# Macaron block on one core: the two leading bf16 parts of the near position bias, stacked in the array's rows and added with a doubled identity

## The chip, the core and the metric

The kernel runs on one core of one Trainium2 chip. The metric is device time in microseconds (us) of one execution, lower being better. The five engines are TensorE (PE, with its weight loads shown as PEld), VectorE (DVE), ScalarE (ACT), GpSimd (POOL) and SyncE (SP), which here issues nearly all DMAs.

## What is computed

Three stages run one after the other over 4 batches of 1024 tokens with 128 channels: half a feed-forward block, an attention with a relative position bias, half a feed-forward block again. Each feed-forward block holds an attention of its own without bias and a mixture of 8 experts, so all three stages have a 16-head attention over 1024 tokens; only the middle one has the bias.

```python
x = x + 0.5 * _L0_ffn_ref(_layernorm(x), ...)
x = x + _L0_attn_ref(_layernorm(x), ...)      # the middle stage
x = x + 0.5 * _L0_ffn_ref(_layernorm(x), ...)

# in _L0_attn_ref
scores = jnp.einsum('bhqd,bhkd->bhqk', q, k) * scale
scores = scores + compute_bias(N, N, rel_bias_table)   # depends on key - query alone
attn = jax.nn.softmax(scores, axis=-1)
```

The bias of a head depends on key minus query, and is constant beyond a distance of 128.

## The kernel before

**Units and steps.** The attention of one batch and four heads (a quad) is a unit: 16 units a stage, 48 in all, numbered u. A unit has 16 steps t, one for each half of the queries (512 columns) and key tile of 128 keys; a step has two half steps, each with two heads. The global step is 16 u + t. All engines run the same loop over the steps; their waits on semaphores bind them together.

**A half step on PE** (`pe_step`). First two products for the row maximum of work that lies 13 steps ahead (`pe_max`, L1024: 48 rows of the array, 128 columns of weights, 512 columns streamed), into one of two double-bank slots that DVE empties (`dve_max`, by a plain maximum, L1379, or by adding a strip of bias and taking the maximum, L1384). Then two products for the transposed scores of two heads (`pe_score`, L1051), one in rows 0 to 63 of the array and one in rows 64 to 127, each into one of three banks that ACT empties with the exponential (L1273). In the middle stage, where the key tile lies near the queries, the near bias follows (`pe_near`, L1072). Then the products of the weights with the values (`pe_pv`, L1089: 128 rows, 9 columns, four heads in four column strips of the array, 8 fp32 passes in all). The negated row maxima come through `carry_max` on SP, which waits for POOL's `pool_parts` (L806 and after) and carries them over DRAM into the rows of the queries.

**The near bias** (`pe_near`, L1072). The bias of a key tile and the queries up to 96 columns to either side is kept as three bf16 parts (`near`, with axes v, s, j, c: two patterns, three parts, four heads, 320 columns). Each part of each key half (64 keys) is added to the scores by a 64 by 64 product with an identity. The four quarters of the array are used by two heads and two key halves: head s, key half `keys` stands in rows `keys ^ s`, so that the four products of one part lie in four quarters. That makes 12 products for a pair of heads:

```python
for part_ in range(3):
    for s in range(2):
        for keys in range(2):
            rows_ = slice((keys ^ s) * P // 2, (keys ^ s) * P // 2 + P // 2)
            mm_ = pe.matmul(bank[keys half], ident_b[rows_, rows_], near[...][rows_, kt % 2, part_, ...])
```

Steps 0 to 4 and 11 to 15 of a unit have the near bias, ten of sixteen.

**Where the parts come from.** During the first stage the table is built once. For each quad, `cut_near` (SP, eight DMAs) loads a cut, `pool_near` (POOL, L795 to L798) reorders it into `near_all[1]`, and `keep_near` (SP, L618, eight DMAs of one step each) stores it to DRAM in the layout that the quarters need. `NEAR_STEPS` sets the steps at which POOL does this: 61, 85, 109, 125 for the four quads. A quad's cuts are issued in the 8 steps that end two before its step, its keeps in the 8 steps from 7 after it. `pool_near` of a quad waits until all keeps of the quad before have landed. In the middle stage `load_near` reads one quad a unit ahead, in eight DMAs. SP, POOL and PE go through their instructions in order, so `pool_near` stands in POOL's way of what comes next there: `pool_heads` (L822, which PE's output projection L1157 waits for) and `pool_parts` (L806).

Of the kernel before, what the change touches and what calls it, by code (L numbers as in the profile page):

```python
# [18 lines left out]
QUADS = H // 4  # L19
KT = N // P  # L20
HALF = 512
# [17 lines left out]
MARGIN = 96  # L39
NEAR = MARGIN + P + MARGIN  # L40
# [115 lines left out]
STRIP_CUTS = 4  # L156

NEAR_STEPS = [8 * w + 5 for w in (WINDOWS - 1, WINDOWS + 2, WINDOWS + 5, WINDOWS + 7)]
CUT_LOADS = 8


UNIT_LOADS, NEAR_LOADS, STRIP_LOADS = (6, 7, 8, 9, 10, 14), (0, 1, 2, 3, 6, 7, 8, 9), (10, 11, 14, 15)
# [120 lines left out]
def stages(nc, k, x, out):  # L283
    c, w = k.consts, k.w
# [2 lines left out]
    near_in = [k.sem(f"a_near_in{p}") for p in range(2)]  # L287
    near_cut, near_set, near_kept = k.sem("near_cut"), k.sem("near_set"), k.sem("near_kept")
    sheared = [k.sem(f"sheared{quad}") for quad in range(QUADS)]
    strips_cut, ident_ready = k.sem("strips_cut"), k.sem("ident_ready")  # L290
    filled, drained, far_added, row_maxed = k.sem("filled"), k.sem("drained"), k.sem("far_added"), k.sem("row_maxed")
    max_turned = k.sem("max_turned")
    max_parts, max_out, max_rows = k.sem("max_parts"), k.sem("max_out"), k.sem("max_rows")
    max_chain, scored, taken, pv = k.sem("max_chain"), k.sem("scored"), k.sem("taken"), k.sem("pv")
# [29 lines left out]
    turned, max_rest = k.sb("max_turned", [P, 32]), k.sb("max_rest", [P, 32])  # L324
    row_parts = k.sb("max_parts", [P, 3, 32], BF16)
    ident_b = k.sb("ident_b", [P, P], BF16)
    strips = [k.sb(f"strips{p}", [P, 4, STRIP], BF16) for p in range(2)]
    near_all = [k.sb(f"near{p}", [P, NEAR_SET * NEAR], BF16) for p in range(2)]
    near = [t[:, :].rearrange("p (v s j c) -> p v s j c", v=2, s=3, j=4) for t in near_all]
# [61 lines left out]
    taken_bank, heads_bank = k.psum[4:7], k.psum[7]  # L391
# [218 lines left out]
    def keep_near(sp, quad, piece):  # L610


        sp.wait_ge(near_set, quad + 1)
        by_head = lambda tile: tile.rearrange("p (o j s c) -> p s (o j) c", s=2, j=2, c=NEAR)
        src, dst = by_head(near_all[1][:, :]), by_head(k.nears[quad])
        s, p = piece % 2, piece // 2 * 32
        at = (p + s * P // 2) % P
        sp.dma_start(dst[at:at + 32, s], src[p:p + 32, s]).then_inc(near_kept, 16)  # L618

    def store_parts(sp, n, b, h):  # L620

# [98 lines left out]
    def sp_between(sp, step):  # L720
# [11 lines left out]
        for quad in range(QUADS):  # L732
            since = step - NEAR_STEPS[quad]
            if -1 - CUT_LOADS <= since < -1:
                cut_near(sp, quad, since + 1 + CUT_LOADS)
            if 7 <= since < 15:
                keep_near(sp, quad, since - 7)
        if step % KT == 2 and KT < step <= STEPS + 2:
            store_heads(sp, step // KT - 1)
# [46 lines left out]
    def pool_near(pool, quad):  # L786

        pool.wait_ge(near_cut, (quad + 1) * CUT_LOADS * 16)  # L790
        if quad:
            pool.wait_ge(near_kept, quad * 8 * 16)
        strip = lambda v, c0, c1: near_one[:, v, :, :, c0:c1].rearrange("p s j c -> p (s j) c")
        from_cut = lambda v, c0, c1: cut[:, c0:c1, v * 12:(v + 1) * 12].rearrange("p c e -> p e c")
        pool.tensor_copy(strip(0, 0, MARGIN), from_cut(1, 0, MARGIN))  # L795
        pool.tensor_copy(strip(0, MARGIN, NEAR), from_cut(0, MARGIN, NEAR))
        pool.tensor_copy(strip(1, 0, MARGIN + P), from_cut(1, 0, MARGIN + P))
        pool.tensor_copy(strip(1, MARGIN + P, NEAR), from_cut(0, MARGIN + P, NEAR)).then_inc(near_set, 1)  # L798
# [257 lines left out]
    def pe_near(pe, u, e):  # L1056

        half, kt = divmod(e // 4, KT)  # L1060
        if e == 0:
            pe.wait_ge(near_in[u % 2], ((u - B * QUADS) // 2 + 1) * len(NEAR_LOADS) * 16)
            pe.wait_ge(ident_ready, 1)
        for part_ in range(3):
            for s in range(2):
                bank = taken_bank[seat["exp", u, e + s] % 3]
                for keys in range(2):
                    rows_ = slice((keys ^ s) * P // 2, (keys ^ s) * P // 2 + P // 2)
                    at = kt * P + keys * P // 2 - MARGIN
                    lo, hi = max(at, half * HALF), min(at + P // 2 + 2 * MARGIN, (half + 1) * HALF)  # L1070
                    c0 = lo - (kt * P - MARGIN)
                    mm_ = pe.matmul(bank[keys * P // 2:(keys + 1) * P // 2, lo - half * HALF:hi - half * HALF],  # L1072
                                    ident_b[rows_, rows_], near[u % 2][rows_, kt % 2, part_, (e + s) % 4, c0:c0 + hi - lo],
                                    start=False, stop=part_ == 2)
                if part_ == 2:
                    mm_.then_inc(scored, 1)

    def pe_pv(pe, step, part_):

# [591 lines left out]
    with nc.Block() as block:  # L1671
        @block.sync
        def _(sp):
# [12 lines left out]
            for step in range(LAST_STEP):  # L1686
                u, t = divmod(step, UNIT_STEPS)
                if u < UNITS:
# [3 lines left out]
                    if t == LAG + 1:  # L1692
                        carry_max(sp, u, 1)
                        if u + 2 < UNITS and is_mid(u + 2) and not is_mid(u):
                            sp.wait_ge(strips_cut, QUADS * STRIP_CUTS * 16)
                            sp.wait_ge(near_kept, QUADS * 8 * 16)
                    if t == LAG + KT + 1 and u + 1 < UNITS:
                        carry_max(sp, u + 1, 0)
                    pace(sp, step)
# [36 lines left out]
        def _(act):  # L1736
# [9 lines left out]
                act.activation(bias[:, n * 512:(n + 1) * 512], k.psum[n][0:H, :], ACT.Copy).then_inc(bias_sb, 1)  # L1746
            act.wait_ge(weights_in, 12 * 16)
            act.activation(tri_b[:, :], tri[:, :], ACT.Copy).then_inc(ident_ready, 1)
            for step in range(LAST_STEP):
                u, t = divmod(step, UNIT_STEPS)  # L1750
                for i in range(2):
# [118 lines left out]
```

## Time and profile before

| | |
|---|---|
| median of 3 runs | 2491.53 us (2486.31 to 2499.0) |
| the profiled execution | 2491.56 us |
| its span in the profile | 2489.8 us |
| PE busy | 2260.1 us, 91% of the span |
| PEld busy | 844.6 us, 34% |
| DVE busy | 1940.7 us, 78% |
| ACT busy | 1947.4 us, 78% |
| POOL busy | 809.2 us, 33% |

Busy time is the union of an engine's instructions. Those of PE are pipelined: two that follow one another overlap, so the duration of one product says less than the distance between the starts of two groups. A shape such as "64*64 64x256" on a product means rows by columns of the array, then rows by streamed columns; x12 is the number of instructions merged in the row.

### The profile page before, as it was taken

To read this page: it belongs to the slowest core of one execution; us is meant where nothing else is said; L and a number is where in the kernel's file an instruction comes from. 1 tells how busy PE (TensorE), PEld (TensorE's weight loads), DVE (VectorE), ACT (ScalarE), POOL (GpSimd) and SP (SyncE) were. 2 spreads that over 40 slices of the span, in tenths; PEclk is the share of its full clock that TensorE was granted. 3 is DMA by queue.
4 is the path that set the end of the run, shared out by engine and by line. 5 is a ranking of instruction groups with operands and counts; after the bars stand their busy time and mean duration, and the time that the engine had idled before them with its cause. 6 is when DMAs were issued, how large, how long until landed. Compare 5 with 4: busy or idle time off the path is not lost. (4 is left out here: it accounts for less than half of the span.)

```text
span 2489.8 us, 62168 instructions
## 1 busy us (share of the span) xinstructions
PE 2260.1 (91%) x24154; PEld 844.6 (34%) x24154; DVE 1940.7 (78%) x3200; ACT 1947.4 (78%) x3559; POOL 809.2 (33%) x1083
## 2 busy tenths in 40 slices
PE   4899898999998999999899999999999999989935
PEld 1232222235421334543233333332222223542425
DVE  7888898985788887578887988998989998569210
ACT  1698798899887778887677877888979989878822
POOL 1363634320634612032353023023062222062153
PEclk7899999999999999999999999999999999999967
DMA  5346443236215445743544444311212113722525
GB/s 151 108 151 195 144 95 96 68 107 171 73 36 139 120 130 151 217 122 104 140 110 144 120 114 114 76 38 57 54 30 79 45 27 107 199 51 67 138 78 144
DMA packets 293533, 268.11 MB, mean 108 GB/s; under 512 B 62220, under 2 KB 238924, under 8 KB 293208
## 3 DMA queue, kind: packets, MB, share of 16 engines
q1 hardware_dynamic: 281976, 255.76, 37.5%
q0 software_dynamic: 11264, 8.40, 1.9%
q8 instruction: 190, 3.11, 0.5%
q14 instruction: 103, 0.84, 0.1%
HBM read 192.30 MB, written 84.02 MB: 111 GB/s over the span
## 5 line engine op out<-in xcount | busy, mean ns | idle before, releaser
L1273 ACT ACTIVATE probs<-psum 128x512 f32<-128x512 f32 x3072 | 1657.7, 599 | 314.2 <-PE psum L1051 169.9
L1379 DVE TENSOR_REDUCE maxes<-psum 128x2 f32<-128x1024 f32 x1216 | 1424.1, 1216 | 266.2 <-PE psum L1024 263.7
L1089 PE MATMUL psum<-probs,v_ones 128*9 128x256 f32 (+1 forms) x11520 | 945.0, 400 | 0.0
L1024 PE MATMUL psum<-k_staged,q_staged 48*128 48x512 bf16 x3072 | 613.2, 395 | 95.6 <-DVE maxes L1379 57.6
L1051 PE MATMUL psum<-q_staged,k_staged 51*128 51x512 bf16 (+1 forms) x3072 | 632.2, 384 | 35.0 <-DMA q_staged<-neg_max 18.7
L1384 DVE CUSTOM_DVE_ANT_0 biased<-psum,strips 128x512 bf16<-128x512 f32 x640 | 411.7, 686 | 110.9 <-PE psum L1024 89.3
L1024 PEld LDWEIGHTS psum<-k_staged,q_staged 48*128 48x128 bf16 x3072 | 147.9, 93 | 776.2 <-DVE maxes L1379 404.7
L806 POOL CAST max_parts<-max_turned 128x32 bf16<-128x32 f32 x96 | 21.4, 223 | 973.1 <-DVE max_turned L1422 973.1
L1051 PEld LDWEIGHTS psum<-q_staged,k_staged 51*128 51x128 bf16 (+1 forms) x3072 | 259.4, 95 | 193.6 <-ACT probs L1273 62.7
L1089 PEld LDWEIGHTS psum<-probs,v_ones 128*9 128x9 f32 x11520 | 171.1, 88 | 384.6 <-issue 301.7
L1072 PE MATMUL psum<-near,ident_b 64*64 64x256 bf16 (+4 forms) x3840 | 149.3, 252 | 0.0
L950 POOL DMA_INDIRECT x_tokens<-expert_out,rows x64 | 100.3, 1567 | 59.3 <-DMA expert_out<-m_out 41.5
L822 POOL TENSOR_TENSOR o_heads_t<-values,weight_recips 128x512 f32<-128x512 f32 x24 | 30.5, 1270 | 266.9 <-DMA weight_recips<-recips 266.9
L1209 PE MATMUL psum<-m_yt,m_w 128*128 128x128 f32 x816 | 104.4, 287 | 7.4 <-ACT m_yt L1351 7.2
L1072 PEld LDWEIGHTS psum<-near,ident_b 64*64 64x64 bf16 x3840 | 75.2, 106 | 88.0 <-issue 88.0
L1209 PEld LDWEIGHTS psum<-m_yt,m_w 128*128 128x128 f32 x816 | 98.5, 200 | 19.3 <-ACT probs L1273 8.5
L1220 PE MATMUL psum<-m_w,m_hidden 128*128 128x128 f32 x816 | 99.6, 279 | 0.0
L1220 PEld LDWEIGHTS psum<-m_w,m_hidden 128*128 128x128 f32 x816 | 93.8, 192 | 13.8 <-ACT m_hidden L1356 11.6
L939 POOL DMA_INDIRECT sorted_tokens<-o_zn,rows x64 | 62.7, 979 | 95.8 <-PE psum L1051 59.8
L1356 ACT ACTIVATE m_hidden<-psum 128x512 f32<-128x512 f32 x102 | 56.2, 596 | 14.7 <-PE psum L1209 14.3
L868 POOL CAST p_part<-p_qk 128x1024 bf16<-128x1024 f32 x22 | 22.8, 1036 | 109.4 <-DMA k_parts<-p_part 79.6
L1280 ACT ACTIVATE heads_t<-psum 128x512 f32<-128x512 f32 x96 | 58.1, 605 | 0.0
(150 smaller groups left out, 1309.0 us busy)
## 6 DMA issues: line engine op xcount, KB each, us to landing
m_w<-in_w SPq DMA_DIRECT2D x204, 256.0 KB, 3.3
near<-bias_near SPq DMA_DIRECT2D x128, 240.0 KB, 3.9
q_staged<-q_parts SPq DMA_DIRECT2D x96, 192.0 KB
k_staged<-k_parts SPq DMA_DIRECT2D x96, 192.0 KB
strips<-bias_strips SPq DMA_DIRECT2D x64, 288.0 KB, 3.4
q_parts<-p_part SPq DMA_DIRECT2D x23, 384.0 KB, 2.6
k_parts<-p_part SPq DMA_DIRECT2D x23, 384.0 KB, 3.3
bias_cuts<-bias_window SPq DMA_DIRECT2D x32, 240.0 KB, 3.3
```

The costliest lines, as they stand in the source:

```text
L939: pool.indirect_dma_start(out=k.sorted[p], out_offset=bass.IndirectOffsetOnAxis(ap=rows[p][:, t:t + 1], axis=0), in_=zn[:, t, :], in_offse ...
L950: pool.indirect_dma_start(out=k.x[:, b * KT + t, :], out_offset=None, in_=k.moved[at % 2], in_offset=bass.IndirectOffsetOnAxis(ap=rows[at ...
L1024: last = pe.matmul(slots[at % 2][:, s, :], k.qst[u % STAGED][rows_, i, qtile * P:(qtile + 1) * P], k.kst[u % STAGED][rows_, i, chunk * HAL ...
L1051: mm_ = pe.matmul(bank[:, :], k.kst[p][rows_, j // 2, kt * P:(kt + 1) * P], k.qst[p][rows_, j // 2, half * HALF:(half + 1) * HALF], start= ...
L1072: mm_ = pe.matmul(bank[keys * P // 2:(keys + 1) * P // 2, lo - half * HALF:hi - half * HALF], ident_b[rows_, rows_], near[u % 2][rows_, kt ...
L1089: last = pe.matmul(heads_bank[32 * j:32 * j + VC, columns], k.v[:, batch_of(u) * KT + kt, u % QUADS * 4 + j, :], probs[:, step % 3 * 4 + j ...
L1209: last = pe.matmul(bank[:, q * P:(q + 1) * P], w1[done % 2][r][:, q * P:(q + 1) * P], y_t[:, r * P:(r + 1) * P], start=True, stop=True)
L1220: last = pe.matmul(bank[:, r * P:(r + 1) * P], hidden[r][:, q * P:(q + 1) * P], w2[done % 2][r][:, q, :], start=q == 0, stop=q == 3)
L1273: act.activation(probs[:, step % 3 * 4 + e % 4, :], bank[:, :], ACT.Exp).then_inc(taken, 1)
L1280: act.activation(heads_t[:, :], heads_bank[:, :], ACT.Copy).then_inc(heads_sb, 1)
L1379: dve.reduce_max(maxes[u % 2][:, half, 2 * i:2 * i + 2, t, chunk], slot, AX.X).then_inc(drained, 1)
L1384: last = dve.tensor_tensor_reduce(out=biased[:, at % 2 * 2 + s, :], in0=slot[:, s, :], in1=strips[u % 2][:, 2 * i + s, first:first + HALF] ...
```

## The change

It rearranges the three parts in `near`. Parts 0 and 1 of a key half now lie one above the other: rows 0 to 63 hold part 0, rows 64 to 127 part 1, and the two key halves take the two places on the s axis that the parts had. The third part keeps its quarters. `pe_near` adds both leading parts by one product of 128 rows and 64 columns with `ident_two`, two identities one above the other (L1086 in the changed kernel); the third part is added in quarters as before (L1093). A pair of heads has 8 products instead of 12.

```diff
-CUT_LOADS = 8
+CUT_LOADS, KEEPS = 8, 10
...
+    ident_two = k.sb("ident_two", [P, P // 2], BF16)
...
     def keep_near(sp, quad, piece):
         sp.wait_ge(near_set, quad + 1)
-        by_head = lambda tile: tile.rearrange("p (o j s c) -> p s (o j) c", s=2, j=2, c=NEAR)
-        src, dst = by_head(near_all[1][:, :]), by_head(k.nears[quad])
-        s, p = piece % 2, piece // 2 * 32
-        at = (p + s * P // 2) % P
-        sp.dma_start(dst[at:at + 32, s], src[p:p + 32, s]).then_inc(near_kept, 16)
+        half = lambda i: slice(i * P // 2, (i + 1) * P // 2)
+        src, dst = (tile.rearrange("p (v s j c) -> p v s j c", v=2, s=3, j=4) for tile in (near_all[1][:, :], k.nears[quad]))
+        if piece < 4:
+            part_, keys = divmod(piece, 2)
+            src, dst = src[half(keys), :, part_], dst[half(part_), :, keys]
+        else:
+            v, which = divmod(piece - 4, 3)
...
+        sp.dma_start(dst, src).then_inc(near_kept, 16)
...
-            if 7 <= since < 15:
+            if 7 <= since < 7 + KEEPS:
                 keep_near(sp, quad, since - 7)
...
         if quad:
-            pool.wait_ge(near_kept, quad * 8 * 16)
+            pool.wait_ge(near_kept, quad * KEEPS * 16)
...
-        for part_ in range(3):
-            for s in range(2):
-                bank = taken_bank[seat["exp", u, e + s] % 3]
-                for keys in range(2):
...
-                    mm_ = pe.matmul(bank[keys * P // 2:(keys + 1) * P // 2, lo - half * HALF:hi - half * HALF],
-                                    ident_b[rows_, rows_], near[u % 2][rows_, kt % 2, part_, (e + s) % 4, c0:c0 + hi - lo],
-                                    start=False, stop=part_ == 2)
-                if part_ == 2:
-                    mm_.then_inc(scored, 1)
+        for s in range(2):
+            bank = taken_bank[seat["exp", u, e + s] % 3]
+            for keys in range(2):
+                lo, hi, c0 = columns(keys)
+                pe.matmul(bank[keys * P // 2:(keys + 1) * P // 2, lo:hi], ident_two[:, :],
+                          near[u % 2][:, kt % 2, keys, (e + s) % 4, c0:c0 + hi - lo], start=False, stop=False)
+        for s in range(2):
+            bank = taken_bank[seat["exp", u, e + s] % 3]
+            for keys in range(2):
+                lo, hi, c0 = columns(keys)
+                rows_ = slice((keys ^ s) * P // 2, (keys ^ s) * P // 2 + P // 2)
+                mm_ = pe.matmul(bank[keys * P // 2:(keys + 1) * P // 2, lo:hi], ident_b[rows_, rows_],
+                                near[u % 2][rows_, kt % 2, 2, (e + s) % 4, c0:c0 + hi - lo], start=False, stop=True)
+            mm_.then_inc(scored, 1)
...
             act.activation(tri_b[:, :], tri[:, :], ACT.Copy).then_inc(ident_ready, 1)
+            for side in range(2):
+                rows_ = slice(side * P // 2, (side + 1) * P // 2)
+                act.activation(ident_two[rows_, :], k.ident[rows_, rows_], ACT.Copy).then_inc(two_ready, 1)
```

On TensorE, at a near half step of the middle stage where both key halves have 256 columns, the order was:

```order
L1024 MATMUL psum<-k_staged,q_staged 128x512 x2
L1051 MATMUL psum<-q_staged,k_staged 128x512 x2
L1072 MATMUL psum<-near,ident_b 64x256 x12
L1089 MATMUL psum<-probs,v_ones 9x256 x4
L1024 MATMUL psum<-k_staged,q_staged 128x512 x2
```

and is now (lines further down by 9 to 19; L1033 is the maximum product, L1060 the score product, L1108 the values):

```order
L1033 MATMUL psum<-k_staged,q_staged 128x512 x2
L1060 MATMUL psum<-q_staged,k_staged 128x512 x2
L1086 MATMUL psum<-near,ident_two 64x256 x4
L1093 MATMUL psum<-near,ident_b 64x256 x4
L1108 MATMUL psum<-probs,v_ones 9x256 x4
L1033 MATMUL psum<-k_staged,q_staged 128x512 x2
```

The twelve products in quarters became four that span all rows and four in quarters, at the same place.

On SyncE, at the end of the keeps of the third quad (quad 2, global steps 122 to 128), the order was (L607 loads the cuts of the fourth quad, L618 keeps the third, L574 and L579 are `carry_max`):

```order
L618 DMA bias_near<-near 384x1x320
L607 DMA near<-bias_cuts 128x960
L653 DMA weight_sums<-heads_0 128x64
L654 DMA values<-heads_0 128x512
L574 DMA neg_max<-max_parts 48x1x32 x4
L579 DMA q_staged<-neg_max 3x4x128 x4
L660 DMA recips<-weight_sums 128x64
L666 DMA weight_recips<-recips 128x1x512
```

and is now (L627 keeps, L608 cuts, L575 and L580 carry):

```order
L627 DMA bias_near<-near 128x2x320
L608 DMA near<-bias_cuts 128x960
L662 DMA weight_sums<-heads_0 128x64
L663 DMA values<-heads_0 128x512
L575 DMA neg_max<-max_parts 48x1x32 x4
L580 DMA q_staged<-neg_max 3x4x128 x4
L627 DMA bias_near<-near 64x2x320 x2
L669 DMA recips<-weight_sums 128x64
L675 DMA weight_recips<-recips 128x1x512
```

The last two keeps of that quad now stand behind a carry of the maxima.

## Rows read from the trace of the kernel before

**Rows 1.** The page: PE's granted clock in 40 slices of the span, in tenths.

```profile
PEclk7899999999999999999999999999999999999967
```

**Rows 2.** Windows: the middle stage; busy us of PE, PEld, DVE, ACT, POOL, then clock.

```profile
817.00:1634.00 817.00, 794.37 (x10390) 304.73 (x10388) 662.02 (x1608) 637.81 (x1162) 223.82 (x314) 1.00 0.47 127
```

**Rows 3.** Waits, 817 to 1634: who waited for whom, us in total, times, longest.

```profile
ACT probs L1273 <- PE psum L1072: 132.7, 294, 6.2
...
DVE biased L1384 <- PE psum L1024: 88.9, 141, 4.2
```

**Rows 4.** Timeline of PE, two half steps with 256 columns (start, length).

```profile
1106.64 0.52 PE L1072 MATMUL psum<-near,ident_b 64*64 64x256 bf16 x12
...
1107.65 0.39 PE L1024 MATMUL psum<-k_staged,q_staged 48*128 48x512 bf16 x2
1107.87 0.38 PE L1051 MATMUL psum<-q_staged,k_staged 63*128 63x512 bf16 x2
1108.19 0.52 PE L1072 MATMUL psum<-near,ident_b 64*64 64x256 bf16 x12
1108.64 0.39 PE L1024 MATMUL psum<-k_staged,q_staged 48*128 48x512 bf16 x2
```

**Rows 5.** Timeline of PE, same group, windows after its first and its second wave.

```profile
1108.32 0.39 PE L1072 MATMUL psum<-near,ident_b 64*64 64x256 bf16 x8
...
1108.43 0.28 PE L1072 MATMUL psum<-near,ident_b 64*64 64x256 bf16 x4
```

**Rows 6.** Timeline of PE, expert products before a maximum product, last two starts.

```profile
1002.96 0.39 PE L1209 MATMUL psum<-m_yt,m_w 128*128 128x128 f32 x2
...
1003.07 0.28 PE L1209 MATMUL psum<-m_yt,m_w 128*128 128x128 f32 x1
...
1003.28 0.39 PE L1024 MATMUL psum<-k_staged,q_staged 48*128 48x512 bf16 x2
```

**Rows 7.** Groups by shape, PE: near products (count, busy us, mean ns).

```profile
L1072 PE MATMUL psum<-near,ident_b 64*64 64x256 bf16 x1536 | 66.8, 277 | 0.0
L1072 PE MATMUL psum<-near,ident_b 64*64 64x224 bf16 x768 | 61.9, 266 | 0.0
...
L1072 PE MATMUL psum<-near,ident_b 64*64 64x96 bf16 x384 | 20.4, 211 | 0.0
```

**Rows 8.** Timeline of PE: groups of 224/160 and of 96/32 columns; the latter's successor.

```profile
1102.14 0.48 PE L1072 MATMUL psum<-near,ident_b 64*64 64x224 bf16 x12
...
1433.23 0.32 PE L1072 MATMUL psum<-near,ident_b 64*64 64x32 bf16 x12
...
1433.48 0.62 PE L1089 MATMUL psum<-probs,v_ones 128*9 128x256 f32 x8
```

**Rows 9.** Timeline: the value products and their loads, second wave; near loads, groups.

```profile
1102.55 0.12 PEld L1089 LDWEIGHTS psum<-probs,v_ones 128*9 128x9 f32 x8 [0.17 <-issue]
...
1102.77 0.40 PE L1089 MATMUL psum<-probs,v_ones 128*9 128x256 f32 x4
...
L1072 PEld LDWEIGHTS psum<-near,ident_b 64*64 64x64 bf16 x3840 | 75.2, 106 | 88.0 <-issue 88.0
```

**Rows 10.** Timeline of SP's DMA issues around the fourth quad's cuts.

```profile
410.05 0.56 SPq L618 DMA_DIRECT2D bias_near<-near  x1
410.64 1.27 SPq L607 DMA_DIRECT2D near<-bias_cuts  x1
...
418.95 0.34 SPq L660 DMA_DIRECT2D recips<-weight_sums  x1
```

**Rows 11.** Timeline of POOL and PE after those cuts.

```profile
414.35 2.17 POOL L795 COPY near<-near 128x1152 bf16<-128x1152 bf16 x1 [7.94 <-DMA near<-bias_cuts]
...
428.41 1.26 POOL L822 TENSOR_TENSOR o_heads_t<-values,weight_recips 128x512 f32<-128x512 f32 x1
...
432.07 1.16 PE L1157 MATMUL psum<-w_proj_ffn,o_heads_t 128*128 128x128 f32 x8
```

**Rows 12.** Groups of the page: DVE's plain maximum (count, busy us, mean ns).

```profile
L1379 DVE TENSOR_REDUCE maxes<-psum 128x2 f32<-128x1024 f32 x1216 | 1424.1, 1216 | 266.2 <-PE psum L1024 263.7
```

More of the change, by code:

```diff
@@ L289, in stages @@
     sheared = [k.sem(f"sheared{quad}") for quad in range(QUADS)]
-    strips_cut, ident_ready = k.sem("strips_cut"), k.sem("ident_ready")
+    strips_cut, ident_ready, two_ready = k.sem("strips_cut"), k.sem("ident_ready"), k.sem("two_ready")
     filled, drained, far_added, row_maxed = k.sem("filled"), k.sem("drained"), k.sem("far_added"), k.sem("row_maxed")
@@ L613, in keep_near @@
         sp.wait_ge(near_set, quad + 1)
-        by_head = lambda tile: tile.rearrange("p (o j s c) -> p s (o j) c", s=2, j=2, c=NEAR)
-        src, dst = by_head(near_all[1][:, :]), by_head(k.nears[quad])
-        s, p = piece % 2, piece // 2 * 32
-        at = (p + s * P // 2) % P
-        sp.dma_start(dst[at:at + 32, s], src[p:p + 32, s]).then_inc(near_kept, 16)
+        half = lambda i: slice(i * P // 2, (i + 1) * P // 2)
[5 more added lines that the diff above has]
+            v, which = divmod(piece - 4, 3)
+            by_head = lambda tile: tile[:, v, 2].rearrange("p (j o) c -> p o j c", o=2)[:, which > 0]
+            src, dst = by_head(src), by_head(dst)
+            if which:
+                src, dst = src[half(which - 1)], dst[half(2 - which)]
+        sp.dma_start(dst, src).then_inc(near_kept, 16)
     def store_parts(sp, n, b, h):
@@ L1063, in pe_near, with columns @@
             pe.wait_ge(ident_ready, 1)
-        for part_ in range(3):
-            for s in range(2):
-                bank = taken_bank[seat["exp", u, e + s] % 3]
-                for keys in range(2):
[L1068 to L1071, printed above, removed]
-                    mm_ = pe.matmul(bank[keys * P // 2:(keys + 1) * P // 2, lo - half * HALF:hi - half * HALF],
-                                    ident_b[rows_, rows_], near[u % 2][rows_, kt % 2, part_, (e + s) % 4, c0:c0 + hi - lo],
-                                    start=False, stop=part_ == 2)
-                if part_ == 2:
-                    mm_.then_inc(scored, 1)
+            pe.wait_ge(two_ready, 2)
+        def columns(keys):
+            at = kt * P + keys * P // 2 - MARGIN
+            lo, hi = max(at, half * HALF), min(at + P // 2 + 2 * MARGIN, (half + 1) * HALF)
+            return lo - half * HALF, hi - half * HALF, lo - (kt * P - MARGIN)
+        for s in range(2):
[12 more added lines that the diff above has]
+            mm_.then_inc(scored, 1)
     def pe_pv(pe, step, part_):
@@ L1695, in _ @@
                             sp.wait_ge(strips_cut, QUADS * STRIP_CUTS * 16)
-                            sp.wait_ge(near_kept, QUADS * 8 * 16)
+                            sp.wait_ge(near_kept, QUADS * KEEPS * 16)
                     if t == LAG + KT + 1 and u + 1 < UNITS:
```

## The prediction

> **What bounds the kernel now.** I read the granted clock first [rows 1]: apart from the two ends it is full speed or one tenth below it, so the clock is not what a change of PE's work meets here. The windows by stage come second [rows 2]: in the middle stage, the only one that has near products, PE is busy 794.37 of 817 us, DVE 662.02 and ACT 637.81. PE can be idle for at most 22.6 us there, so what is added to PE's work in that stage is added to the time. The waits say the same from the other side [rows 3]: the exponentials wait 132.7 us for the near products, and DVE waits 88.9 us for the maximum products. Both engines have room; PE has none.
>
> Busy time of pipelined products counts overlaps, so from here on only distances between starts are used. In a half step with 256 near columns [rows 4] the near group starts at 1106.64, then come the values, the maximum products at 1107.65, the scores at 1107.87 and the next near group at 1108.19. That is 1.55 us a half step. The second group has 0.45 us (no value products stand behind it, and the next maximum products start at 1108.64).
>
> The near group itself goes in three waves of four products, one in each quarter [rows 4, 5]: starts at 1108.19, 1108.32, 1108.43, and the next work at 1108.64. Inside a shape the waves are 0.11 apart, the first one 0.13 because its weights are loaded with nothing in flight. The step from the last wave to another shape is 0.21. The same is seen from the maximum products to the scores (both half the rows, all columns: 0.22 for 512 columns) and from the scores to the near quarters (0.32 for the same 512 columns). So **each change of the array's division costs about 0.10 us** on top of the streaming.
>
> **The change, part by part.**
>
> *The near products.* Counting waves, nothing is gained. Two column halves with all rows fill the array as four quarters do. So the stacked products of head 0 are one wave, those of head 1 a second (same columns, they can't run together), the third part in quarters a third. Three waves before, three now, each as wide. The number of products falls from 12 to 8, but the waves are spaced by their columns, not by their number.
>
> What is new is one more change of division in every group, from all rows by 64 columns to 64 by 64. Here columns stay and rows change. A change of rows alone stands in the trace where expert products (128 by 128) are followed by maximum products (48 rows, so a half, by 128) [rows 6]: 1002.96 to 1003.07 is 0.11 within the shape, 1003.07 to 1003.28 is 0.21 across. So rows alone cost 0.10 as well. New group: 0.13 (head 0 to head 1), 0.21 (to the quarters), 0.21 to the values, and up to 0.02 because that last wave is now also the first of its shape. Sum 0.55 to 0.57 instead of 0.45: 0.10 to 0.12 more, taken as 0.11. The number of groups is the count of products over 12 [rows 7]: with 256 columns 1536/12 = 128; with 224 and 160 (768 each) 128; with 96 and 32 (384 each) 64; together 320. The cost does not depend on the width. **320 x 0.11 = 35 us** (32 to 38). ACT's next exponential and DVE's next maximum shift along; they have room and hide none of it, since PE is what they wait for.
>
> Nearest rows for bounds: below, a change of rows that costs nothing, 0; above, stacked products that don't run side by side (under the rivals).
>
> *The weight loads of the second stacked wave.* It uses the same rows and columns as the first. The value products are such a case: they use all 128 rows, and all eight loads are done within 0.12 us from 1102.55, long before the second wave starts at 1102.77 [rows 9]. So I take them as hidden, at 0. The Trainium skill says otherwise: "TensorE: Matmul & The Clock Gate", Part 3, "The mechanism", has loads overlap running products only when the row group differs. By that the sum would hold the load once more in the open, which is the second rival below.
>
> *Keeps: ten DMAs instead of eight a quad.* The bytes are the same; eight more issues in all at 0.56 us [rows 10] lie in the idle time of SP. But two of them matter by place. The keeps of quad 2 run over steps 116 to 125, and the fourth call of `pool_near` is at step 125 and now needs all ten. The last two stand behind the carry of step 124, as the order shows. SP was through that carry when it issued L660 at 418.95 [rows 10]. So the two go out at about 418.9 and 419.5 and land some 3 us later (the last cut, issued at 410.64, let POOL start at 414.35, 3.7 us after [rows 10, 11]), say at 422.9. `pool_near` starts then instead of at 414.35: **8.5 us later**. Behind it on POOL stand `pool_heads` (L822, 428.41 to 429.67) and `pool_parts`. PE reaches L1157, which needs L822, at 432.07 [rows 11]. L822 would end at 438.2, so PE stands for 6.1 us. The maxima behind it are late by the same and meet PE where it already lost that time, so they add nothing. DVE has up to two full slots to work off while PE stands, 1.2 us each [rows 12], so of the 6.1 between 3.7 and 6.1 reach the end: **5 us**, bounds 0 (a later slack eats it) and 8.5 (all of POOL's delay). The same check for the other quads: steps 76 and 77 against 85, 100 and 101 against 109, 140 and 141 with no call after; they cost nothing.
>
> *The rest.* Two small copies on ACT at the start and one more wait there are done long before the first near group at 817 us. Loads of `near` in the middle stage are unchanged. 0.
>
> **Sum.** 2491.6 (the profiled execution, equal to the median of 2491.5) + 35 + 5 = 2532, 1.6% more.
>
> **Rivals.**
>
> 1. *A change of rows is free here*, or stacked and quartered waves merge across the boundary. Then only the 5 us of POOL stay: 2497. Against it: 0.10 in rows 6, and 0.10 in all other changes of rows 4.
>
> 2. *The loads of the second stacked wave are not hidden*: it starts when the first has streamed (0.11) and its weights are in (106 ns, [rows 9]), at 0.22 instead of 0.13. That is 0.09 x 320 = 29 more: 2561. Against it: the loads of L1089.
>
> 3. *The two column halves don't run side by side*, so four stacked waves instead of two. Extra 2 x 0.11 at 256 columns, 2 x 0.07 at 224/160 (the narrower one is added), 0.03 at 96/32: 128 x 0.22 + 128 x 0.14 + 64 x 0.03 = 48 more, 2580. Against it: the four column strips of L1089 run as one wave.
>
> 4. *The number of products decides, and the kernel gets faster.* If a group's time were its 12 pairs of load and product, 8 pairs would take a third off: 0.15 of 0.45, 0.14 of 0.41 (1102.14 to the values' first load at 1102.55), 0.08 of 0.25 [rows 4, 8, 9]. That gives 128 x 0.15 + 128 x 0.14 + 64 x 0.08 = 42 us less, 2455 with the 5 of POOL. It decides from the point where a wave's columns take less time than four pairs take to issue. For it: the narrow group needs 0.25 with hardly any columns. Against it: with the same 12 pairs groups last 0.25, 0.41 and 0.45 as the columns grow, 0.11 a wave is the streaming time of 256 columns (512 take 0.22, rows 4), and the narrow group is a fifth of all. The Trainium skill, "TensorEngine Tiling (Array Packing)", "Instruction Overhead", gives each product some 60 cycles; an estimate by it is 4 x 25 ns x 320 = 32 us less, if they never overlapped.
>
> **How the numbers follow.** Forecast 0.77, with a range of its own from 2515 to 2547 (32 to 38 for the change of division, loosened for waits that the longer half step absorbs, and 0 to 8.5 for POOL). Rival 1 0.08, rival 2 0.06, rival 3 0.04, rival 4 0.05. The range goes up over rival 2, which leaves rivals 1, 3 and 4 outside, 0.17, with a little at the lower edge: 2510 to 2562. A measurement of this kernel tells about 0.5%, 12.5 us, from no change. Faster is rival 4, 0.05; within 0.5% is rival 1 without its upper tail, 0.08; the rest is slower, 0.87.
>
> **What would show it.** In the changed profile: near half steps with 256 columns some 1.65 us apart instead of 1.55; the stacked waves 0.13 apart, then 0.21 to the quarters and 0.21 to 0.23 to the values; DVE's wait for the maximum products up by about 30 us and ACT's wait for the near products too; the middle stage about 850 us long, the last stage unchanged. In the first stage `pool_near` near 423 with its wait ended by a keep, and PE waiting for L822 for about 6 us. I am wrong if the step between the stacked wave and the quarters is 0.11 (rival 1), if head 1 starts 0.22 after head 0 (rival 2), if the four stacked products show four starts 0.11 apart (rival 3), or if a narrow group shrinks (rival 4).

## The result, and the profile after

The changed kernel takes 2527.07 us (median of 4 runs, 2526.26 to 2527.32) against 2490.51 of the kernel before (2486.31 to 2499.0) in the same comparison: a ratio of 1.0142, 95% interval 1.0115 to 1.0169, so 36.6 us slower. The forecast was 2532, slower, with 2510 to 2562 as its range.

PE's part of the page of the changed kernel, to be read beside the table of before:

```profile
PE 2294.8 (91%) x22874; PEld 850.3 (34%) x22874; DVE 1944.5 (77%) x3200; ACT 1949.0 (77%) x3561; POOL 811.4 (32%) x1083
...
PEclk7899998999999999999999999999999999999967
```

PE lost 1280 products and gained 34.7 us of busy time; DVE and ACT do what they did, within 4 us. The granted clock differs in one slice, the seventh (379 to 442 us), which shows 8 instead of 9; what lies there is told below. The middle stage, 823 to 1672 us now (columns as in [rows 2]):

```profile
823.00:1672.00 849.00, 831.64 (x9116) 310.81 (x9112) 663.64 (x1610) 638.69 (x1162) 224.47 (x314) 1.00 0.45 122
```

It lasts 849 us instead of 817. PE's sequence at 256 columns, to be read against [rows 4, 5] (L1060 scores, L1086 stacked products, L1093 quarters, L1108 values, L1033 maximum products). The line with x2 comes from a window behind the end of the first stacked wave, so its start is that of the second:

```profile
1122.72 0.38 PE L1060 MATMUL psum<-q_staged,k_staged 63*128 63x512 bf16 x2
1123.04 0.41 PE L1086 MATMUL psum<-near,ident_two 128*64 128x256 bf16 x4
...
1123.17 0.28 PE L1086 MATMUL psum<-near,ident_two 128*64 128x256 bf16 x2
...
1123.38 0.30 PE L1093 MATMUL psum<-near,ident_b 64*64 64x256 bf16 x4
1123.61 0.62 PE L1108 MATMUL psum<-probs,v_ones 128*9 128x256 f32 x8
1124.16 0.39 PE L1033 MATMUL psum<-k_staged,q_staged 48*128 48x512 bf16 x2
1124.39 0.38 PE L1060 MATMUL psum<-q_staged,k_staged 63*128 63x512 bf16 x2
1124.70 0.41 PE L1086 MATMUL psum<-near,ident_two 128*64 128x256 bf16 x4
```

Starts: 1123.04, then +0.13 to the second stacked wave, +0.21 to the quarters, +0.23 to the values: 0.57 us, where it was 0.45. The half step is 1123.04 to 1124.70, 1.66 us, where it was 1.55. The other two widths grew by the same 0.12, though their columns differ:

```profile
1119.79 0.38 PE L1086 MATMUL psum<-near,ident_two 128*64 128x160 bf16 x4
1120.10 0.29 PE L1093 MATMUL psum<-near,ident_b 64*64 64x160 bf16 x4
1120.32 0.62 PE L1108 MATMUL psum<-probs,v_ones 128*9 128x256 f32 x8
...
839.05 0.27 PE L1086 MATMUL psum<-near,ident_two 128*64 128x96 bf16 x4
839.25 0.23 PE L1093 MATMUL psum<-near,ident_b 64*64 64x96 bf16 x4
839.42 0.40 PE L1108 MATMUL psum<-probs,v_ones 128*9 128x256 f32 x4
```

That is 0.53 against 0.41 and 0.37 against 0.25. The engines that wait for PE wait longer (823 to 1672 us, to be read against [rows 3]):

```profile
ACT probs L1292 <- PE psum L1093: 163.3, 296, 4.7
...
DVE biased L1403 <- PE psum L1033: 110.3, 162, 4.3
```

Both are up, by 31 and 21 us. The other term, POOL and SP in the first stage, to be read against [rows 10, 11]:

```profile
411.80 0.47 SPq L608 DMA_DIRECT2D near<-bias_cuts  x1
...
419.06 1.23 SPq L580 DMA_DIRECT2D q_staged<-neg_max  x4
421.46 1.32 SPq L627 DMA_DIRECT2D bias_near<-near  x2
...
424.52 2.21 POOL L804 COPY near<-near 128x1152 bf16<-128x1152 bf16 x1 [16.08 <-DMA bias_near<-near]
...
438.66 1.25 POOL L831 TENSOR_TENSOR o_heads_t<-values,weight_recips 128x512 f32<-128x512 f32 x1
...
440.06 2.04 PE L1176 MATMUL psum<-w_proj_ffn,o_heads_t 128*128 128x128 f32 x8 [5.12 <-POOL o_heads_t L831]
```

The last two keeps go out behind the carry, `pool_near` waits 16.08 us for them and starts at 424.52 instead of 414.35, and PE stands 5.12 us in front of the output projection (L1176). The granted clock falls while PE stands there. The same stretch in both kernels, the changed one first:

```profile
437.00:443.80 6.80, 3.74 (x20) 2.04 (x20) 3.08 (x4) 1.30 (x3) 4.73 (x8) 0.50 0.18 45
```

```profile
437.00:443.80 6.80, 5.61 (x66) 1.51 (x67) 6.76 (x15) 5.50 (x11) 5.51 (x7) 1.00 0.50 112
```

From 437.0 to 443.8 us TensorE ran at the lower of its two clock levels (0.50, 1.2 GHz), in the kernel before at the upper one (1.00, 2.4 GHz). PE had stood from 434.94 to 440.06. So the eight products of L1176 take 2.04 us where L1157 took 1.16 [rows 11], and what follows them up to 443.8 is slow too. PE loses more than it waits: taking the starts of the same score products in both traces, the changed kernel is 2.8 us behind at 434.01 (431.21 before) and 9.6 behind from 444.14 on (434.48 before), so 6.8 us go at this place.

### The profile page after: what moved, and what is told of

Read it like the earlier page. It is cut to its first block and busy times, and to the rows that moved or that the text cites. A ratio compares the mean times of both kernels' runs of the same rounds, so it can differ in the third digit from the quotient of the medians.

```text
span 2524.4 us, 59621 instructions
## 1 busy us (share of the span) xinstructions
PE 2294.8 (91%) x22874; PEld 850.3 (34%) x22874; DVE 1944.5 (77%) x3200; ACT 1949.0 (77%) x3561; POOL 811.4 (32%) x1083
## 3 DMA queue, kind: packets, MB, share of 16 engines
q1 hardware_dynamic: 275960, 255.76, 36.6%
## 5 line engine op out<-in xcount | busy, mean ns | idle before, releaser
L1108 PE MATMUL psum<-probs,v_ones 128*9 128x256 f32 (+1 forms) x11520 | 943.0, 399 | 0.0
L1033 PE MATMUL psum<-k_staged,q_staged 48*128 48x512 bf16 x3072 | 612.8, 395 | 92.3 <-DVE maxes L1398 59.0
L1060 PE MATMUL psum<-q_staged,k_staged 51*128 51x512 bf16 (+1 forms) x3072 | 631.9, 384 | 33.9 <-DMA q_staged<-neg_max 18.5
L1033 PEld LDWEIGHTS psum<-k_staged,q_staged 48*128 48x128 bf16 x3072 | 147.8, 93 | 770.7 <-DVE maxes L1398 424.1
L1060 PEld LDWEIGHTS psum<-q_staged,k_staged 51*128 51x128 bf16 (+1 forms) x3072 | 259.6, 95 | 192.8 <-ACT probs L1292 61.8
L1108 PEld LDWEIGHTS psum<-probs,v_ones 128*9 128x9 f32 x11520 | 171.0, 88 | 365.7 <-issue 259.0
L1086 PE MATMUL psum<-near,ident_two 128*64 128x256 bf16 (+4 forms) x1280 | 119.1, 259 | 0.0
L831 POOL TENSOR_TENSOR o_heads_t<-values,weight_recips 128x512 f32<-128x512 f32 x24 | 30.5, 1271 | 266.7 <-DMA weight_recips<-recips 266.7
L1093 PE MATMUL psum<-near,ident_b 64*64 64x256 bf16 (+4 forms) x1280 | 91.0, 267 | 0.0
L1086 PEld LDWEIGHTS psum<-near,ident_two 128*64 128x64 bf16 x1280 | 45.1, 108 | 87.2 <-issue 87.2
```

The costliest lines, as they stand in the source:

```text
L1033: last = pe.matmul(slots[at % 2][:, s, :], k.qst[u % STAGED][rows_, i, qtile * P:(qtile + 1) * P], k.kst[u % STAGED][rows_, i, chunk * HAL ...
L1060: mm_ = pe.matmul(bank[:, :], k.kst[p][rows_, j // 2, kt * P:(kt + 1) * P], k.qst[p][rows_, j // 2, half * HALF:(half + 1) * HALF], start= ...
L1086: pe.matmul(bank[keys * P // 2:(keys + 1) * P // 2, lo:hi], ident_two[:, :], near[u % 2][:, kt % 2, keys, (e + s) % 4, c0:c0 + hi - lo], s ...
L1093: mm_ = pe.matmul(bank[keys * P // 2:(keys + 1) * P // 2, lo:hi], ident_b[rows_, rows_], near[u % 2][rows_, kt % 2, 2, (e + s) % 4, c0:c0 ...
L1108: last = pe.matmul(heads_bank[32 * j:32 * j + VC, columns], k.v[:, batch_of(u) * KT + kt, u % QUADS * 4 + j, :], probs[:, step % 3 * 4 + j ...
```

## The experiments

Two theories stood against each other for the middle stage. By the first, the added change of the array's division costs about 0.12 us a group, whatever the products. By the second, the stacked products are themselves slow (their columns don't run side by side, or the loads of the second wave lie open). A third possibility is that a second kind of weights in a group costs the time, whatever its shape. For the first stage the theory is that the place of the last two keeps makes POOL late; its rival is that nothing of it reaches the end.

In the table, "middle" is from the first to the last start of the near products in the profiled execution, as their groups give it, and "ahead" the first of them. The kernel before has 817.0 and 817.2 (to 1634.2), the changed kernel 823.3 and 849.0.

| run | ahead | middle | span | ratio to before, 95% |
|---|---|---|---|---|
| changed | 823.3 | 849.0 | 2524.4 | 1.0142 (1.0115 to 1.0169) |
| changed, again | 829.3 | 849.7 | 2533.3 | 1.0150 (1.0134 to 1.0166) |
| keeps in eight steps | 817.9 | 848.3 | 2519.9 | 1.0110 (1.0093 to 1.0127) |
| the same, again | 830.6 | 845.6 | 2531.7 | 1.0123 (1.0104 to 1.0143) |
| before, keeps late | 821.2 | 817.6 | 2492.8 | 1.0003 (0.9991 to 1.0015) |
| stacked, third left out | 830.9 | 792.9 | 2478.0 | 0.9903 (0.9886 to 0.9921) |
| quarters, third left out | 819.4 | 793.9 | 2468.1 | 0.9901 (0.9884 to 0.9918) |
| third by whole rows | 830.5 | 841.1 | 2527.4 | 1.0121 (1.0092 to 1.0149) |
| quarters first | 832.7 | 848.4 | 2537.1 | 1.0150 (1.0121 to 1.0178) |
| column strips | 820.1 | 767.6 | 2441.7 | 0.9808 (0.9779 to 0.9836) |
| column strips, again | 814.2 | 771.6 | 2439.2 | 0.9801 (0.9781 to 0.9821) |

The middle column is steady to some 4 us. The column ahead of it is not: the two profiles with the keeps in eight steps differ there by 12.7 us, though they are of one kernel. So what the middle stage says is read from single profiles, and what the first stage says only from the place itself.

**The third part left out, in both layouts.** In the changed kernel the loop over the quarters goes, and the stacked products end the group; in the kernel before the loop over the parts is cut to two.

```diff
-                pe.matmul(... ident_two[:, :], ..., start=False, stop=False)
-        for s in range(2):
...
-                mm_ = pe.matmul(... ident_b[rows_, rows_], ..., start=False, stop=True)
+                mm_ = pe.matmul(... ident_two[:, :], ..., start=False, stop=True)
```

> The changed kernel, leaving out the third bf16 part of the near bias, so only the four stacked products of a pair are left. Division theory: no second change of division, so a group of 256 columns lasts 0.13 + 0.20 = 0.33 us, as long as two waves of quarters in the sibling run that leaves out the third part of the kernel before; the middle stage is as long in both, and this one is longer than the sibling by the 6 us of POOL alone. From 2527: 320 x 0.12 less for the division and its first load, and 128 x 0.11 + 128 x 0.10 + 64 x 0.04 = 29 less for the wave, so 2460 if nothing else becomes the bound; DVE's maxima may hold it at up to 2475. Rival (the stacked products are slow themselves): groups of 0.43 or more, and the middle stage 30 us longer than the sibling's.

```diff
-        for part_ in range(3):
+        for part_ in range(2):
...
-                                    start=False, stop=part_ == 2)
+                                    start=False, stop=part_ == 1)
```

> The kernel before, leaving out the third bf16 part of the near bias: eight products in quarters for a pair, two waves. Both theories: a group of 256 columns lasts 0.13 + 0.20 = 0.33 us instead of 0.45, 29 us less by 128 x 0.11 + 128 x 0.10 + 64 x 0.04, so 2462; up to 2475 if DVE's maxima become the bound. It is the measure for the run with stacked products.

Measured: 2471.43 us (2466.8 to 2479.8) with stacked products, 2469.28 (2466.91 to 2472.22) with quarters, 2494.71 for before. PE in the one with stacked products, then in the one with quarters (the values are L1101 and L1089):

```profile
1107.39 0.41 PE L1086 MATMUL psum<-near,ident_two 128*64 128x256 bf16 x4
1107.73 0.62 PE L1101 MATMUL psum<-probs,v_ones 128*9 128x256 f32 x8
```

```profile
1094.52 0.41 PE L1072 MATMUL psum<-near,ident_b 64*64 64x256 bf16 x8
1094.86 0.62 PE L1089 MATMUL psum<-probs,v_ones 128*9 128x256 f32 x8
```

Four stacked products take 0.34 us, eight in quarters 0.34 us, and the middle stages are 792.9 and 793.9 us long. So the stacked products are not slow, they are not quick either, and the second wave's weights are hidden. The whole loss in the middle stage appears only where both kinds stand in one group. Halving the number of products at equal waves gains nothing, in the narrow groups (96 and 32 columns) neither, where both take some 0.21 us; that is the end of the rival by which their number decides. One expectation was missed: the run with stacked products has the late keeps too and was to be longer by 6 us for POOL. It is longer by 2.2, and the two sets of runs overlap.

**The order turned round.** The changed kernel with the quarters ahead of the stacked products.

```diff
-                pe.matmul(bank[...], ident_two[:, :], near[...], start=False, stop=False)
+                pe.matmul(bank[...], ident_b[rows_, rows_], near[...], start=False, stop=False)
...
-                mm_ = pe.matmul(bank[...], ident_b[rows_, rows_], near[...], start=False, stop=True)
+                mm_ = pe.matmul(bank[...], ident_two[:, :], near[...], start=False, stop=True)
```

> The changed kernel with the third part's quarters ahead of the stacked products. The number of changes of division is the same, each pair of neighbours is another (scores 64 x 128 to quarters 64 x 64, to stacked 128 x 64, to values 128 x 32: after the quarters only the rows change, and then only the columns). Theory (each change costs 0.1 whatever it is): groups of 0.57 us at 256 columns, 2527. Rival (only the way from whole rows to half rows costs, because the upper half must drain): groups back near 0.47, 2495 to 2500.

Measured: 2537.93 us (2535.04 to 2538.87) with 2499.33 before, ratio 1.0150, middle stage 848.4. The group at 256 columns (quarters L1087, stacked L1093):

```profile
1132.77 0.30 PE L1087 MATMUL psum<-near,ident_b 64*64 64x256 bf16 x4
1133.00 0.41 PE L1093 MATMUL psum<-near,ident_two 128*64 128x256 bf16 x4
1133.34 0.40 PE L1108 MATMUL psum<-probs,v_ones 128*9 128x256 f32 x4
```

Again 0.57: 0.23 and 0.34. The way from half rows to whole rows costs what the way back costs. It is the number of changes that counts. The wave that stands alone in its division costs 0.23, as the one at the end of the group did in the changed kernel.

**The third part by whole rows.** A wave more against a change of division less.

```diff
-                mm_ = pe.matmul(..., ident_b[rows_, rows_],
-                                near[u % 2][rows_, kt % 2, 2, ...], start=False, stop=True)
+                mm_ = pe.matmul(..., ident_b[:, side],
+                                near[u % 2][:, kt % 2, 2, ...], start=False, stop=True)
```

> The changed kernel, its third part added by products of 128 rows and 64 columns too, with an identity in one half of the rows and zeros in the other: four waves of one division instead of two waves, a change of division, one wave. Division theory: a wave more (0.11, 0.10, 0.045 us by width) against a change less (0.12), so groups of 0.55, 0.48 and 0.28 us instead of 0.57, 0.53 and 0.37; 128 x 0.02 + 128 x 0.05 + 64 x 0.09 = 15 us less than the changed kernel, about 2512 where it has 2527. Rival (the extra time comes with the stacked products or their weight loads): groups longer than in the changed kernel by a wave each, 20 us more, 2547.

Measured: 2529.2 us (2527.88 to 2532.18) with 2499.33 before.

```profile
1128.30 0.41 PE L1086 MATMUL psum<-near,ident_two 128*64 128x256 bf16 x4
1128.54 0.39 PE L1093 MATMUL psum<-near,ident_b 128*64 128x256 bf16 x4
1128.86 0.40 PE L1108 MATMUL psum<-probs,v_ones 128*9 128x256 f32 x4
...
846.02 0.27 PE L1086 MATMUL psum<-near,ident_two 128*64 128x96 bf16 x4
846.11 0.27 PE L1093 MATMUL psum<-near,ident_b 128*64 128x32 bf16 x4
846.31 0.62 PE L1108 MATMUL psum<-probs,v_ones 128*9 128x256 f32 x8
```

The group takes 0.56 us with four waves, a little under the 0.57 with three waves and one more change. The narrow group takes 0.29, well under the 0.37. The sign is the division theory's; the rival wanted a wave on top. The run also answers the third possibility: `ident_b` is still a second kind of weights, for the same places in PSUM as before, but in the same division it costs no more than its two waves (0.34 to 0.56, 0.11 each). The size is a miss. The middle stage fell from 849.0 to 841.1, so 8 us where 15 were expected: the groups take 0.56, 0.50 and 0.29 us instead of 0.55, 0.48 and 0.28, which leaves 10 to 11, and the rest is not traced. The ratio of 1.0121 is not told apart from the changed kernel's. Here a change of division and a wave of 256 columns cost nearly the same.

**The keeps.** The ten keeps in eight steps (the changed kernel), and the eight keeps two steps later (the kernel before).

```diff
-            if 7 <= since < 7 + KEEPS:
-                keep_near(sp, quad, since - 7)
+            if 7 <= since < 15:
+                for piece in ((0,), (1,), (2,), (3,), (4,), (5,), (6, 7), (8, 9))[since - 7]:
+                    keep_near(sp, quad, piece)
```

> The changed kernel with its ten keeps issued in eight steps, so that none stands behind the carry of step 124. POOL theory: pool_near of the last quad starts near 415 to 417 again instead of 424.5, its wait is ended by the cuts, PE no longer waits 5.1 us for L831, and the middle stage begins 6 to 7 us earlier than in the changed kernel; the whole is 3 to 6 us under it, 2521 to 2524. Rival (the delay of the first stage has another source, the layout of the keeps): the first stage stays as long as in the changed kernel and the time stays 2527.

```diff
-            if 7 <= since < 15:
-                keep_near(sp, quad, since - 7)
+            if 9 <= since < 17:
+                keep_near(sp, quad, since - 9)
```

> The kernel before, with its eight keeps two steps later, so that the last two stand behind the carry of step 124; the products are those of before. POOL theory: pool_near of the last quad starts about 8 to 10 us later than 414.35, PE waits 5 to 6 us for L822, the middle stage begins 6 to 7 us later than before; the whole is 3 to 6 us longer, 2494 to 2497. Rival: the delay is absorbed before the middle stage, 2491. Near groups stay 0.45 us at 256 columns in both.

Measured: 2521.33 us (2519.19 to 2524.01) and 2495.13 us (2490.68 to 2504.0), both beside 2494.71 for before. POOL at the call in question, with the keeps in eight steps, then with the late keeps in the kernel before, where PE's wait follows:

```profile
413.52 2.17 POOL L805 COPY near<-near 128x1152 bf16<-128x1152 bf16 x1 [8.04 <-DMA near<-bias_cuts]
```

```profile
419.81 2.22 POOL L795 COPY near<-near 128x1152 bf16<-128x1152 bf16 x1 [15.49 <-DMA bias_near<-near]
...
PE psum L1157 <- POOL o_heads_t L822: 6.6, 1, 6.6
```

The mechanism is switched off by the one edit and on by the other: with eight steps the wait is ended by the cuts again and PE no longer waits for L831; with late keeps alone the kernel before gets both. All profiles agree on this. In the six with late keeps PE waits 4.8 to 6.6 us at the output projection, a stretch of 6.8 us at the lower clock level begins there (434 to 440 us), and the scores behind it start 6.8 to 8.8 us later than in the kernel before, counted from just ahead of the place. In the other five that difference is 0.0.

What it is worth at the end is another matter. The middle stage begins 5.4 us earlier than in the changed kernel with the one edit (817.9) and 4.2 us later than in the kernel before with the other (821.2), where 6 to 7 were expected, but that start differs by more between profiles of one kernel. The late keeps changed the time of the kernel before by 0.4 us, with an interval of the ratio from 0.9991 to 1.0015, that is 2.2 us less to 3.7 more. The theory wanted 3 to 6 us more. Its 2494 to 2497 seem to hold the 2495.13, but they were counted from a kernel before at 2491.5, which has 2494.71 in this comparison. So this run speaks for the rival, "absorbed", more than for the theory. The changed kernel speaks the other way: its ratio is 1.0142 with the late keeps and 1.0110 with eight steps, 8 us apart where 3 to 6 were expected, from two comparisons. To come closer, three kernels ran once more on one chip:

> The changed kernel itself once more, on the same chip as the next two runs, so that they can be compared at half a per cent. Ratio to the kernel before 1.014 as measured first; near groups of 0.57, 0.53 and 0.37 us, PE waiting about 5 us for L831.

> The ten keeps in eight steps, again, beside the changed kernel. POOL theory: 4 to 7 us less than the changed kernel in the run above, ratio to the kernel before 1.011 to 1.012. Rival (the early delay is eaten by later waits): within 2 us of it.

Measured: 2535.15 us (2533.2 to 2536.85) for the changed kernel and 2529.92 (2525.56 to 2533.51) with the keeps in eight steps, 5.2 us less, with 2499.36 for before. The two sets of runs overlap by 0.3 us, and the intervals of the ratios (1.0134 to 1.0166, 1.0104 to 1.0143) overlap. In this pair of profiles the middle stage even began later with the early keeps (830.6 against 829.3). So the loss stands in the place where it arises. That it reaches the end is likely for the changed kernel, by two pairs of medians, and not shown; in the kernel before it did not show at the end at all.

**Three parts in column strips.** If the number of waves and the number of changes of division are the price, then both can be cut: all three parts of 32 keys, one above the other in 96 rows, times three identities, into 32 columns. Two heads and four key strips make eight products of at most 224 columns in two waves, and the values behind them use strips of 32 columns as well. The near tile has the axes p, q (key strip), v, j, c; the twelve keeps of a quad go out in eight steps. Where a strip has no columns in the half, one column of zeros is added instead.

```diff
-CUT_LOADS, KEEPS = 8, 10
+CUT_LOADS, KEEPS = 8, 12
+STRIPS, BLOCK = 4, 2 * MARGIN + P // 4
...
+        part_, q = divmod(piece, 4)
+        src = near_all[1][:, :].rearrange("p (s e c) -> p s e c", s=3, c=NEAR)[q * 32:q * 32 + 32, part_, :, q * 32:q * 32 + BLOCK]
+        dst = k.nears[quad].rearrange("p (q e c) -> p q e c", q=STRIPS, c=BLOCK)[part_ * 32:part_ * 32 + 32, q]
...
+        for s in range(2):
+            for q in range(STRIPS):
+                at = kt * P + q * 32 - MARGIN
+                lo, hi = max(at, half * HALF), min(at + BLOCK, (half + 1) * HALF)
+                if hi > lo:
+                    moving = blocks[u % 2][0:96, q, kt % 2, (e + s) % 4, lo - at:hi - at]
+                else:
+                    lo, hi, moving = half * HALF, half * HALF + 1, none[0:96, :]
+                mm_ = pe.matmul(bank[q * 32:q * 32 + 32, lo - half * HALF:hi - half * HALF], ident_two[0:96, :],
+                                moving, start=False, stop=True)
+            mm_.then_inc(scored, 1)
```

> A version meant to beat both: the three parts of 32 keys one above the other in 96 rows, added by products of 96 rows and 32 columns with three identities; four key strips and two heads make eight products of at most 224 columns. Two waves instead of three, and no change of division towards the value products, which use 32-column strips of all rows too. Division theory: groups of about 0.22, 0.20 and 0.12 us instead of 0.45, 0.41 and 0.25, 65 us less PE in the middle stage, of which DVE's maxima (1.2 to 1.3 us a half step) let 45 to 60 through: 2435 to 2450 against 2494 before. If 96 rows by 32 columns is another division than that of the values, 0.1 us a group more: 2470. Rival (the number of rows or strips decides, not the division): no gain.

> The three parts in column strips, again: ratio to the kernel before 0.981 plus or minus 0.003, some 80 us under the changed kernel.

Measured: 2449.98 us (2443.52 to 2454.62) with 2499.33 before, then 2444.56 (2441.01 to 2453.76) with 2499.36 before: ratios 0.9808 and 0.9801, 2% faster than the kernel before, some 3.5% faster than the changed one. PE (scores L1056, near L1081, values L1096, maximum products L1029):

```profile
1086.67 0.40 PE L1056 MATMUL psum<-q_staged,k_staged 63*128 63x512 bf16 x2
1087.00 0.38 PE L1081 MATMUL psum<-near,ident_two 96*32 96x224 bf16 x8
1087.21 0.61 PE L1096 MATMUL psum<-probs,v_ones 128*9 128x256 f32 x8
1087.75 0.39 PE L1029 MATMUL psum<-k_staged,q_staged 48*128 48x512 bf16 x2
1087.97 0.40 PE L1056 MATMUL psum<-q_staged,k_staged 63*128 63x512 bf16 x2
1088.30 0.38 PE L1081 MATMUL psum<-near,ident_two 96*32 96x224 bf16 x8
...
1097.42 0.38 PE L1081 MATMUL psum<-near,ident_two 96*32 96x224 bf16 x8
1097.73 0.39 PE L1029 MATMUL psum<-k_staged,q_staged 48*128 48x512 bf16 x2
```

The middle stage of the same run, by windows:

```profile
820.00:1588.00 768.00, 735.03 (x9128) 282.23 (x9126) 656.61 (x1608) 635.07 (x1163) 224.18 (x314) 0.99 0.47 123
```

The group takes 0.21 us for two waves, so there is no 0.10 in front of the values. The last two lines show it within the kernel: the same group with the maximum products right behind it (48 rows by 128 columns) takes 0.31. So 96 rows by 32 columns and 128 by 9 count as one division here. The half step is 1.30 us. The middle stage is 767.6 us long, 50 less than before; PE is busy 735.03 of 768 us and still the busiest engine, though it is now idle for 33.

## Why the prediction was right

*What bounds the kernel.* Right. PE's middle stage grew by 31.8 us, DVE's and ACT's work did not move, and both wait longer by what was said (DVE 110.3 against 88.9 for the biased maxima and 60.6 against 49.0 for the plain ones, together 33; ACT 31). The middle stage was forecast at 850 and is 849.0.

*The waves.* Right in each piece: three waves remain, 0.13 between the stacked ones, 0.21 to the quarters, 0.23 to the values. The half step was forecast at 1.65 and is 1.66.

*A change of division costs 0.10, with the lone wave's 0.02 on top.* Right in kind, a little small in size: 0.11 was taken from 0.10 to 0.12, and 0.12 was measured at all three widths. It was read where rows alone change [rows 6]; the type of the products changes there too (f32 to bf16), so the reading was less clean than the prediction took it. The runs show the cause: without the third part the loss is gone, with the order turned round it is the same, and with the third part in whole rows it gives way to the price of a wave. 320 x 0.12 is 38.4 us.

*All of it passes through.* Here the forecast was too simple, and the error went against that of the size. It took PE's idle time in the middle stage, 22.6 us, as no room at all. But PE waits in it for work that isn't its own, and a later PE waits less: its idle time is 17.4 us now (849.00 less 831.64). The same score products, set side by side in both traces, show where. At each of the 320 near half steps they move apart by 0.12 us, at the others by nothing, but for fewer than twenty places, which together take 6.6 us back. That is the whole difference between 38.4 and 31.8. Half of it is in four lines, PE's longest waits in the middle stage of the kernel before and of the changed one:

```profile
PE psum L1024 <- DVE maxes L1384: 10.4, 22, 0.8
PE psum L1024 <- DMA q_staged<-far_rows: 5.0, 1, 5.0
```

```profile
PE psum L1033 <- DVE maxes L1403: 8.6, 21, 0.6
PE psum L1033 <- DMA q_staged<-far_rows: 3.4, 1, 3.4
```

The second line of each is one wait, of the first maximum products of a late unit, for rows that come when they come. With the small waits for the exponentials, for `neg_max` and for L822, PE waits 21.0 us before and 15.8 now, so 5.2 of the 6.6 us are waits that became shorter. The other 1.4 are not traced in full.

*The weight loads of the second stacked wave.* Right: 0.13 between the waves, not 0.22. The Trainium skill, "TensorE: Matmul & The Clock Gate", Part 3, "The mechanism", says that loads overlap running products only when the row group differs; by this the load would lie in the open, and this trace does not agree, neither here nor at L1089. The same section also names a background weight buffer as a second way to load ahead, and that the trace does not contradict.

*POOL.* Right in kind: the two keeps behind the carry, PE's wait for L831, no second wait for the maxima. The keeps went out 2.5 us later than forecast (421.46 for 418.9), since the stretch ahead had slipped by as much, but landed sooner after that: `pool_near` started 1.6 later (424.52 for 422.9), and PE waited 5.1 for 6.1 us. What the prediction left out is the clock. It read the 40 slices as "full speed or one tenth below" and set it aside, but a slice is a mean over 62 us and hides short stretches at the lower level. PE's standing brought one, and the place cost 6.8 us, not 5.1. That the 5 us of the sum reach the end was assumed. It is not shown, and the kernel before with late keeps speaks against it. That term is right by luck as far as the runs tell.

*The rest.* From the last near product to the end of the span it was 855.6 us before and is 852.1 us now. It was forecast at no change. The other ten runs have 853.4 to 856.0 there, the changed kernel's second profile 854.3, so the 852.1 lies a little under the spread, and nothing shows it to be the change.

*The sum.* 35 and 5 were forecast and 36.6 measured. In the profile it is 6.3 ahead of the middle stage, 31.8 in it, 3.5 less behind it: 34.6 of span. That the total came out this close is in part luck: a term too small by 3.4 (35 for 38.4) met 6.6 us that were absorbed, and the parts outside the middle stage are of the size of the spread between profiles. The range could have been tighter on the side of rivals 2 and 3, which the rows of L1089 already spoke against.

## What to carry to other kernels

Count waves of the array and changes of its division, not products: at equal waves, four products that fill all rows and eight in quarters took the same 0.34 us, while one more division of the array inside a group cost 0.12 us each time. Before taking it that a busy engine passes on all that is added, look at what it waits for in its idle time: waits for others shrink as it gets later. A layout that stacks parts pays where it takes a wave out or makes neighbours share a division, as the column strips did. And where a row of DMAs grows by two steps, see what the queue does in those steps and who waits for the last of them.

## What was not expected of the hardware

Products of 96 rows by 32 columns run into products of 128 rows by 9 columns without the 0.10 us that they pay in front of 48 rows by 128 columns (0.21 against 0.31 us from the start of the group). So a pair of neighbouring shapes needs not be equal to be free; nor are the maximum and the score products, 48 and 63 rows by 128 columns, which follow each other in 0.22 us, the time of 512 columns. And one more change of division cost the same 0.12 us, within 0.01, whichever way the rows changed, and in groups of 256, of 224 and 160, and of 96 and 32 columns alike.
